# Setup of a graph layer reordered: row credits first, statistics in a row, node turns over six banks

## The chip, the cores and the metric

The kernel runs on one core of a Trainium2 chip. The metric is the time of one execution in microseconds (us), the median of the runs shown. Before the change it is 634.7 us (three runs, 634.36 to 635.47).

The engines of the core are named as in the profile: PE is TensorE, DVE is VectorE, ACT is ScalarE, POOL is GpSimd, SP is SyncE. PEld is TensorE's weight load. A name with a "q" (DVEq, POOLq) is that engine's instruction queue at work on registers, semaphores or DMA issues rather than on data.

## The reference

A graph layer (a message per edge, summed at its target node, then two dense layers with batch normalisation) is followed by a mixture of 16 experts. Only the first part matters here:

```python
x0 = layernorm(x)                              # x: 1250 nodes x 512
msg = relu(x0[src] + edge_attr @ W_e + b_e)    # 21250 edges, edge_attr: 21250 x 64
aggr = segment_sum(msg, dst, num_segments=1250)
h = (1.0 + eps) * x0 + aggr
h = silu(batchnorm(h @ W1 + b1, g1, beta1))    # W1: 512 x 1024
h = h @ W2 + b2                                # W2: 1024 x 512
x = x + silu(batchnorm(h, g2, beta2))
# then experts: gate, top 156 tokens for each of 16 experts, two dense layers each, weighted sum
```

The edges come sorted by `dst`. Source nodes are arbitrary, so rows of `x0` are gathered.

## The kernel before

Each engine has a program of its own, in the order in which it is written, and the programs meet at semaphores. An engine does its instructions strictly in that order, so whatever waits holds up all that stands behind it on the same engine.

**Setup.** SP issues the loads of `x` in five groups of two tiles (125 rows each), then `W_e`, the first block of edge attributes and `eps`. ACT issues the loads of `dst` (two forms), `src` and the bias `b_e` (`be_all`). Per group `g` of two tiles: `statistics(g)` on DVE (L812: two BN_STATS, two BN_AGGR), `deviations(g)` on ACT (L540, a square root), `norm_terms(g)` on DVE (L823: reciprocal and mean term), `normalise(g)` on ACT (L545, two tiles into `xn`), `table(g)` on DVE (L830: 64 times `xn` plus scaled bias, written over `xs`), and then SP writes these rows to `node_rows` in DRAM (L366 to L370). ACT's order is `deviations(g+1)` ahead of `normalise(g)`. On DVE the five groups follow one another nearly whole: `statistics(2)` stands behind `table(0)`, `statistics(3)` behind `table(1)`, `statistics(4)` behind `table(2)` (L843 to L887). `statistics(1)` stands behind the scaling of `be_all` (L845), which waits for that load.

Between these, DVE works out from `dst` where each block of edges begins (`sb_base`, `shift`, `base_i`) and whether one pass over the edges is enough (`n_pass`, through `outside`, `n_out`, a product on PE at L1287 and `pass_ready`). With the data here one pass is run.

The normalised nodes are also turned (features by nodes) into `aggT`, times 1 + eps. PE turns tile `t` into `bank[t % 2]` (`node_transposes`, L1275), even tiles are copied by ACT (L558 to L562) and odd ones by DVE (`node_columns`, L890). Both copies stand behind the last step of the tables on their engine, and tile `t` of PE waits for the copy of tile `t - 2`. Then the small vectors `vecA`, `vecB` are turned (L1290 to L1292) and copied by DVE (L899, L900). SP issues their loads and that of `gate_s` behind the writes of `node_rows`; the four loads of `W1` (0.5 MB each) follow them (L366 to L381).

**Edge steps.** There are 34 steps of five tiles of 128 edges, 167 tiles in all. For tile `t`: POOL gathers 128 rows of `node_rows` into `row(t)`, one of 26 places (L474); PE computes `edge_attr @ W_e` for two tiles at a time into PSUM (`edge_pair`, L1316); DVE adds the gathered row (L952); ACT applies relu into `msg` (L599); PE sums the messages into a window of 64 nodes with a one-hot matrix (`fold`, L1300). Per step ACT copies the sum (`sum_copy`, L574), PE turns it (`turn_sum`, L1308) and DVE adds it into `aggT` at a column that it reads from memory (`accumulate`, L905):

```python
dve.wait_ge(sum_turned, 1 + w * SB + (i + 1))
dve.wait_ge(acc_done, 1 + w * SB + i)
base = dve.value_load(base_i[0:1, bass.ds(w * SB + (i + 2), 1)], min_val=0, max_val=N - 1)
```

DVE does `accumulate(i - 1)` between its fourth and its fifth add of step `i`. In steps 4 to 7 ACT and DVE each also split a quarter of `W1` into two halves (`W1_high` L579, `W1_low` L929). In steps 10 to 33, PE computes one of 24 partial products with `W1` per step (`part_product`, L1337), ACT copies it out (`part_copy`, L586, line L589) and DVE takes its statistics (`part_statistics`, L939, line L942).

POOL may gather a row when `node_rows` is complete (`tab_out`), `pass_ready` is given, and `row_used` allows it. The first increment of `row_used` comes from DVE (L973), as the last thing ahead of its edge steps:

```python
dve.sem_inc(row_used, 1)
dve.sem_inc(acc_done, 1)
run_steps(dve, n_pass, SB, step)
```

## Time and profile before

| | us |
|---|---|
| median of three runs | 634.7 |
| the profiled execution, whole | 632.95 |
| its span, first to last instruction | 631.0 |
| first edge product of PE starts | 43.15 |
| edge steps end (last sum added) | about 301 |
| batch normalisation, second layer, experts | the remaining 330 |

Rows of the trace give the start of an instruction in us from the span's start and its duration. "[idle before <-releaser]" is how long the engine sat idle just ahead of it, and what ended that. The chain of waits is followed back from the last instruction, at each step to what released it; only time on it sets the end.

### The profile page before, as it was taken

How to read it: one execution, taken by the hardware profiler on the slowest of the kernel's cores; microseconds unless marked ns; L12 is line 12 of the kernel's file. 1: busy time of each engine (PE TensorE's matmuls, PEld its weight loads, DVE VectorE, ACT ScalarE, POOL GpSimd, SP SyncE). 2: the span in 40 equal slices, each digit the busy share in tenths (PEclk: the TensorE clock that was granted, in tenths of full speed). 3: DMA queues.
4: the chain of work that ended last, by engine and by line, in shares of the span. 5: the costliest groups of instructions: out<-in, count | busy, mean ns of one | idle time of the engine just before them, and what ended most of it. 6: DMA issues, size and time to landing. Idle time of an engine off the chain costs nothing.

```text
span 631.0 us, 11762 instructions
## 1 busy us (share of the span) xinstructions
PE 495.0 (78%) x4023; PEld 318.0 (50%) x4023; DVE 392.5 (62%) x961; ACT 324.2 (51%) x660; POOL 255.9 (41%) x245
## 2 busy tenths in 40 slices
PE   1068866799989998998899976811499999999990
PEld 1032221233434333334446535610499999999990
DVE  4747655666666675765579746577747666675530
ACT  2425544555554554554486219534046676675750
POOL 2027777777777765400000000000334655556431
PEclk9977978899999998999999997755589999999995
DMA  9487777777777775611667505740058999984331
GB/s 219 122 276 235 225 220 217 221 227 229 228 230 219 219 220 170 188 43 58 211 220 187 157 0 184 232 178 0 21 152 254 299 278 270 302 234 64 60 41 21
DMA packets 48944, 112.44 MB, mean 178 GB/s; under 512 B 7145, under 2 KB 7565, under 8 KB 48886
## 3 DMA queue, kind: packets, MB, share of 16 engines
q0 software_dynamic: 18992, 54.02, 31.6%
q1 hardware_dynamic: 29399, 57.16, 29.0%
q10 hardware_dynamic: 494, 0.52, 0.4%
q8 instruction: 32, 0.52, 0.3%
q14 instruction: 27, 0.21, 0.1%
HBM read 98.88 MB, written 12.79 MB: 177 GB/s over the span
## 4 chain that ended last, share of the span: by engine, by line
PE 62%; DVE 13%; ACT 10%; issue 6%; DMA 3%; DVEq 3%; POOL 1%; SPq 1%; ACTq 1%; POOLq 0%
PE bank L1333 19%; PE bank L1514 11%; PE bank L1303 10%; PE bank L1324 8%; DVE bank L952 4%; ACT big L599 3%; PE bank L1540 2%; PE bank L1312 2%; DVEq L909 2%; PE bank L1495 2%; PE bank L1504 1%; DVE rows_z L1154 1%; PE bank L1383 1%; DMA big<-in_L_gnn_b_e 1%; ACT rows_z L680 1%
## 5 line engine op out<-in xcount | busy, mean ns | idle before, releaser
L1303 PE MATMUL bank<-big,edge_home 128*64 128x256 f32 x668 | 111.5, 426 | 35.2 <-ACT big L599 35.2
L599 ACT ACTIVATE big<-bank 128x512 f32<-128x512 f32 x167 | 99.5, 596 | 71.7 <-DVE bank L952 68.4
L484 POOL DMA_INDIRECT big<-token_rows,idx x32 | 37.6, 1174 | 221.9 <-DVE idx L1212 214.5
L474 POOL DMA_INDIRECT pair<-node_rows,edge_home x97 | 96.3, 992 | 34.6 <-issue 28.0
L1333 PE MATMUL bank<-big,pair 128*128 128x156 f16 (+2 forms) x1056 | 106.5, 260 | 1.1 <-DVE big L1011 0.9
L1333 PEld LDWEIGHTS bank<-big,pair 128*128 128x128 f16 x1056 | 80.9, 97 | 24.5 <-issue 1.4
L474 POOL DMA_INDIRECT big<-node_rows,edge_home x70 | 67.8, 969 | 62.3 <-DVEq L973 37.9
L1303 PEld LDWEIGHTS bank<-big,edge_home 128*64 128x64 f32 x668 | 35.8, 142 | 93.5 <-issue 58.5
L1324 PE MATMUL bank<-edge_home 64*128 64x512 f16 x501 | 74.0, 403 | 3.4 <-DVE edge_home L926 3.4
L493 POOL DMA_INDIRECT out<-rows_z,idx x32 | 51.0, 1593 | 45.2 <-issue 26.3
L952 DVE TENSOR_TENSOR bank<-pair,bank 128x512 f32<-128x512 f32 x97 | 64.3, 687 | 6.1 <-PE bank L1324 5.3
L952 DVE TENSOR_TENSOR bank<-big,bank 128x512 f32<-128x512 f32 x70 | 46.5, 688 | 11.2 <-PE bank L1324 6.4
L912 DVE TENSOR_TENSOR aggT<-bank,aggT 128x256 f32 x34 | 14.4, 425 | 52.3 <-PE bank L1312 50.9
L731 ACT ACTIVATE big<-bank,colB 128x156 f32<-128x156 f32 x64 | 21.5, 388 | 46.2 <-PE bank L1514 46.2
L1324 PEld LDWEIGHTS bank<-edge_home 64*128 64x128 f16 x501 | 18.5, 97 | 49.5 <-issue 37.1
L1333 PE MATMUL bank<-rows_z 128*128 128x250 f16 x288 | 35.8, 273 | 0.0
L1333 PEld LDWEIGHTS bank<-rows_z 128*128 128x128 f16 x288 | 26.5, 98 | 12.5 <-issue 9.7
L1514 PE MATMUL bank<-big,raw 128*128 128x156 f32 x192 | 29.9, 313 | 0.5 <-ACT big L725 0.5
L1200 DVE TENSOR_SCALAR big<-iota_slot,slot 125x156 f16<-125x156 f16 x160 | 28.8, 265 | 0.0
L589 ACT ACTIVATE xs_home<-bank,colA 128x250 f32<-128x250 f32 x18 | 8.5, 470 | 39.4 <-PE bank L1333 39.4
L1514 PEld LDWEIGHTS bank<-big,raw 128*128 128x128 f32 x192 | 27.9, 202 | 0.8 <-ACT big L725 0.8
L1280 PE MATMUL bank<-ident,rows_z 125*128 125x125 f32 x40 | 8.8, 383 | 20.9 <-ACT aggT L560 12.6
(222 smaller groups left out, 778.5 us busy)
## 6 DMA issues: line engine op xcount, KB each, us to landing
raw<-in_L_ffn_w SPq DMA_DIRECT2D x12, 1024.0 KB, 8.5
edge_home<-in_L_ffn_w SPq DMA_DIRECT2D x6, 1024.0 KB, 8.2
pair<-in_L_ffn_w SPq DMA_DIRECT2D x6, 1024.0 KB, 9.7
edge_home<-in_edge_attr SPq DMA_DIRECT2D x19, 320.0 KB, 4.1
xs_home<-in_x SPq DMA_DIRECT2D x10, 448.0 KB
xs_home<-in_L_ffn_w SPq DMA_DIRECT2D x4, 1024.0 KB, 8.2
aggT<-in_L_ffn_w SPq DMA_DIRECT2D x4, 1024.0 KB, 10.6
node_rows<-xs_home SPq DMA_DIRECT2D x5, 448.0 KB
```

Of the source, the lines that this page charges most:

```text
L474: pool.indirect_dma_start(row(t), None, node_rows, bass.IndirectOffsetOnAxis(src_i[:, t:t + 1], 0)).then_inc(row_in[t % RR], 16)
L484: pool.indirect_dma_start(xg[e % XR][:, a, :], None, token_rows, bass.IndirectOffsetOnAxis(idx[:, e, a:a + 1], 0)).then_inc(xg_in[e % XR], 16)
L493: pool.indirect_dma_start(out, bass.IndirectOffsetOnAxis(idx[:, e, a:a + 1], 0), yw[e % YR][:, a, :], None, compute_op=ALU.add).then_inc(y ...
L599: act.activation(msg[:, t % MR, :], bank[t % PB][0:Q, :], ACT.Relu, scale=1.0 / E_SCALE).then_inc(msg_ready, 1)
L731: act.activation(h32[e % 2][:, f, :], bank[2 + half][:, f % 2 * K:(f % 2 + 1) * K], ACT.Gelu_apprx_tanh, bias=colB[:, e * HK + f:e * HK + ...
L912: dve.tensor_tensor(window, bank[6 + i % 2][:, 0:HK * WIN] .rearrange("p (k a n) -> p a k n", k=HK // 2, a=2), window, ALU.add).then_inc(a ...
L952: dve.tensor_tensor(bank[t % PB][0:Q, :], row(t), bank[t % PB][0:Q, :], ALU.add).then_inc(row_used, 1)
L1200: last = dve.tensor_scalar(pick[e % 2][:, t, :], iota_slot[:], slot[:, e, t:t + 1], None, ALU.is_equal)
L1303: done = pe.matmul(bank[6 + b][a * WIN:(a + 1) * WIN, 0:H // 2], onehot[b][:, j, :], msg[:, t % MR, a * (H // 2):(a + 1) * (H // 2)], star ...
L1324: last = pe.matmul(bank[t % PB][0:Q, :], attr16[u % 2][side, i, c * Q:(c + 1) * Q], We16[side, j, :], start=(p == 0), stop=(p == 2), skip_ ...
L1333: last = pe.matmul(bk, weights(i, k), values(j, k), start=(begin and p == k == 0), stop=(end and p == 2 and k == n - 1), skip_group_check= ...
L1514: last = pe.matmul(bank[2 + half][:, f % 2 * K:(f % 2 + 1) * K], e32[e % RH][:, 0, k, f * 128:(f + 1) * 128], xT[e % 2][:, k, :], start=(k ...
```

## The change

The diff is cut to what differs in work or order. Renamed constants (`FG`, `HB`, `PAIRS`, `ZSTART`, `part_at`) have the values that stood there as numbers (2, 256, 5, steps 9, 17, 25), so the schedule of the partial products is the same; `W1` is split one step earlier (steps 3 to 6). Tables for later passes (`shift` and `base_i` for 20 further passes) are gone; the values are remade at the start of a pass by `bases(w)`.

```diff
@@ SP: small loads ahead of the writes of node_rows
+            for v, k in ((b1, F1), (g1, F1), (beta1, F1), (b2, HK), (g2, HK), (beta2, HK)):
+                sp.dma_start(vecA[o:o + k, :], v.rearrange("(k p) -> k p", p=128)).then_inc(vec_in, 16)
+            sp.dma_start(vecB[0:EX * HK, :], ...); sp.dma_start(vecB[EX * HK:, :], ...)
+            sp.dma_start(gate_s[:], gate_t).then_inc(vec_in, 16)
             for g in range(NT // XG):
                 sp.wait_ge(tab_ready, g + 1)
...
             for u in range(1, AR):
                 load_attr(u)
-            (the same nine loads)
             for k in range(HK):
                 sp.dma_start(W1_32[:, k, :], W1_t[:, k, :]).then_inc(w1_in, 16)
@@ POOL
-            pool.iota(shift[:, SB:], [[WIN, NWIN + 1], [0, SB]], base=0, channel_multiplier=0,
+            pool.iota(pass_add[:, 1:], [[WIN, NWIN]], base=0, channel_multiplier=0,
-            pool.iota(base_i[:, 2 + SB:2 + SB * (1 + NWIN)], ...); two memsets of base_i
+            three memsets of pass_add and pass_mul
@@ ACT and DVE, node columns; PE, node transposes
-                               bank[t % 2][:, 0:HK * P]
+                               bank[NB[t % 6]][:, 0:HK * P]        # NB = (0, 1, 2, 5, 6, 7)
-                if t >= 2:
-                    pe.wait_ge(xt_sb[t % 2], t // 2)
+                if t >= 6:
+                    pe.wait_ge(xt_sb[t % 2], (t - 6) // 2 + 1)
-            for t in range(2):
+            for t in range(5):
                 node_transposes(t)
             pe.wait_ge(base_ready, 7)
@@ DVE, setup
+            def be_scaled():
+                dve.wait_ge(be_in, 32)
+                dve.tensor_scalar(be_all, be_all, E_SCALE, None, ALU.mult).then_inc(be_in, 1)
+            dve.sem_inc(row_used, 1)
+            dve.sem_inc(acc_done, 1)
             dve.wait_ge(sorted_in, 32)
...
             statistics(0)
-            dve.wait_ge(be_in, 32)
-            dve.tensor_scalar(be_all, be_all, E_SCALE, None, ALU.mult)
             dst_f copy
+            statistics(1)
             norm_terms(0)
             early
-            dve.wait_ge(iotas, 9)
             dve.wait_ge(base_ps, 1)
-            dve.tensor_copy(base_i[0:1, 2:2 + SB], bank[3][0:1, 0:SB])
             dve.tensor_copy(shift[:, 0:SB], bank[3][0:Q, 0:SB]).then_inc(base_ready, 1)
-            statistics(1), outside, norm_terms(1), outside >= WIN, table(0), n_out, statistics(2), n_out + early,
-            norm_terms(2), table(1), n_pass_f, statistics(3), n_pass_i, norm_terms(3), table(2), dst_left,
-            statistics(4), norm_terms(4), table(3), eps1, dst_left, memset aggT, table(4)
+            statistics(2), norm_terms(1), outside, statistics(3), norm_terms(2), be_scaled, outside >= WIN,
+            wait be_in 33, table(0), statistics(4), norm_terms(3), n_out, table(1), norm_terms(4), n_out + early,
+            table(2), n_pass_f, table(3), n_pass_i, table(4), dst_left, eps1, dst_left, memset aggT,
+            wait iotas 10
             node_columns(1), (3), (5), (7), (9)
@@ DVE, edge steps
             def accumulate(w, i):
+                base = dve.value_load(base_i[0:1, i:i + 1], min_val=0, max_val=N - 1)
                 dve.wait_ge(sum_turned, 1 + w * SB + (i + 1))
                 dve.wait_ge(acc_done, 1 + w * SB + i)
-                base = dve.value_load(base_i[0:1, bass.ds(w * SB + (i + 2), 1)], min_val=0, max_val=N - 1)
...
+            def bases(w):
+                dve.tensor_scalar(shift[:], shift[:], pass_mul[:, bass.ds(w, 1)], pass_add[:, bass.ds(w, 1)],
+                                  ALU.mult, ALU.add).then_inc(based, 1)
+                dve.wait_ge(based, w * 2 + 1)
+                dve.tensor_copy(base_i[:], shift[0:1, :]).then_inc(based, 1)
+                dve.wait_ge(based, w * 2 + 2)
             def columns_hot(w, i):
-                                         scalar=shift[:, bass.ds(w * SB + i, 1)],
+                                         scalar=shift[:, i:i + 1],
             def step(w, i):
                 if i == 0:
+                    bases(w)
                     columns_hot(w, 0)
...
-            dve.sem_inc(row_used, 1)
-            dve.sem_inc(acc_done, 1)
             run_steps(dve, n_pass, SB, step)
```

## Rows read from the trace of the kernel before

**Rows 1.** Busy time by stage: start:end, length, PE, PEld, DVE, ACT, POOL, clock, DMA, GB/s.
```profile
0.00:16.40 16.40, 2.49 (x10) 2.04 (x10) 7.48 (x28) 3.31 (x6) 3.26 (x14) 1.00 0.92 218
...
43.20:77.10 33.90, 28.19 (x182) 9.55 (x182) 20.62 (x34) 17.11 (x31) 25.88 (x27) 0.84 0.80 252
77.10:114.60 37.50, 25.69 (x149) 8.11 (x147) 22.10 (x34) 18.25 (x31) 28.97 (x29) 0.83 0.73 212
...
130.60:300.50 169.90, 154.04 (x1124) 65.92 (x1121) 109.29 (x197) 90.96 (x173) 95.77 (x99) 0.98 0.62 185
```

**Rows 2.** Chain of waits, setup: start, us, what held the end.
```profile
3.17 7.75 DMA big<-in_L_gnn_b_e
...
30.61 1.09 DVE xs_home L833
...
37.01 2.17 DMA gate_s<-in_L_ffn_gate_weight
...
40.94 0.89 issue
...
43.30 4.97 DMA big<-node_rows,edge_home
```

**Rows 3.** Timeline of DVE in the setup: start, us, line, operation.
```profile
6.33 1.27 DVE L817 BATCH_NORM_STATS2 stats<-xs_home 125x6 f32<-125x512 f32 x2
7.63 0.25 DVE L820 BATCH_NORM_AGGREGATE mean_var<-stats 125x2 f32<-125x6 f32 x2
10.95 0.43 DVE L845 TENSOR_SCALAR big<-big 125x512 f32<-125x512 f32 x1 [3.07 <-DMA big<-in_L_gnn_b_e]
...
27.49 0.17 DVE L826 RECIPROCAL rstd<-std 125x2 f32<-125x2 f32 x1 [0.27 <-ACT std L542]
...
30.53 1.16 DVE L833 SCALAR_TENSOR_TENSOR xs_home<-rows_z,big 125x1024 f32<-125x1024 f32 x1
...
38.85 0.74 DVE L892 TENSOR_SCALAR aggT<-bank,eps 128x500 f32<-128x500 f32 x1 [0.80 <-PE bank L1280]
...
42.28 0.82 DVE L926 TENSOR_TENSOR edge_home<-edge_home 128x640 f16<-128x640 f32 x1
```

**Rows 4.** Timeline of ACT in the setup, one group of two tiles.
```profile
18.18 0.20 ACT L542 ACTIVATE std<-mean_var 125x2 f32<-125x2 f32 x1 [3.01 <-DVE mean_var L820]
18.30 1.50 ACT L549 ACTIVATE rows_z<-xs_home,shift_mean,rstd 125x512 f32<-125x512 f32 x2
```

**Rows 5.** Timeline of PE: turns of six node tiles, and the first edge products.
```profile
32.48 5.37 PE L1280 MATMUL bank<-ident,rows_z 125*128 125x125 f32 x24 [0.37 <-DVE aggT L892]
...
43.15 2.74 PE L1324 MATMUL bank<-edge_home 64*128 64x512 f16 x12 [3.43 <-DVE edge_home L926]
```

**Rows 6.** Line L467 in POOL's queue, right behind the wait for `node_rows`: ns, start.
```profile
L467 POOLq TENSOR_LOAD <-n_pass_i x1: 507/507/507, 36.3 to 36.3; - x1
```

**Rows 7.** Timeline, POOL's 1st, 24th, 31st gather; DVE waiting for one.
```profile
41.83 1.16 POOL L474 DMA_INDIRECT big<-node_rows,edge_home  x1 [37.92 <-DVEq L973]
...
71.31 0.95 POOL L474 DMA_INDIRECT pair<-node_rows,edge_home  x1 [0.31 <-issue]
...
74.69 1.35 DVE L952 TENSOR_TENSOR bank<-pair,bank 128x512 f32<-128x512 f32 x2 [0.60 <-DMA pair<-node_rows,edge_home]
...
80.22 1.58 POOL L474 DMA_INDIRECT big<-node_rows,edge_home  x1 [0.30 <-issue]
```

**Rows 8.** Chain of waits in step 7, around the sum's way into `aggT`.
```profile
104.00 0.63 PE bank L1312 x2
...
105.47 0.07 DVE aggT L912
```

**Rows 9.** Timeline of ACT, DVE and PE in a step with a partial product.
```profile
145.74 0.47 ACT L589 ACTIVATE xs_home<-bank,colA 128x250 f32<-128x250 f32 x1 [1.57 <-PE bank L1333]
...
146.25 0.42 DVE L942 BATCH_NORM_STATS2 st<-xs_home 128x6 f32<-128x250 f32 x1
...
148.02 0.65 PE L1303 MATMUL bank<-big,edge_home 128*64 128x256 f32 x4 [0.40 <-ACT big L599]
```

More of the change, by code:

```diff
@@ L47, in gnn_ffn_kernel @@
     ZPARTS = 3
-    ZSTEPS = 8
-    ZHEAD = SB - ZPARTS * ZSTEPS
+    SLOPE, OFFSET = 33.0, 14.0
+    ZSTART = (9, 17, 25)
+    ZOFF = (0, 1, 2, 3, 4, 5, 6, 7)
+    ZLAG = 0
+    assert all(s * SLOPE - OFFSET >= (c + 1) * ZC for c, s in enumerate(ZSTART))
+    part_at = {ZSTART[q // F1] + 1 + ZOFF[q % F1]: q for q in range(ZPARTS * F1)}
+    assert max(part_at) + ZLAG < SB and all(max(ZOFF) + 1 + ZLAG + s <= z for s, z in zip(ZSTART, ZSTART[1:]))
+    W1_FIRST = ZSTART[0] - 6
     YC = [(0, 250), (250, 375), (625, 625)]
@@ L225, in gnn_ffn_kernel @@
         silu = [aggT[:, i, 0:CH[2][1]] for i in range(HK)]
-        half = 2 * J * H
+        half = MR * H
         rows = big[0:Q, 0:half].rearrange("p (s h) -> p s h", h=H)
@@ L236, in row @@
             s = t % RR
-            return rows[:, s, :] if s < 2 * J else late_rows[(s - 2 * J) // 8][:, (s - 2 * J) % 8, :]
+            return rows[:, s, :] if s < MR else late_rows[(s - MR) // 8][:, (s - MR) % 8, :]
         msg = big[0:Q, half:2 * half].rearrange("p (s h) -> p s h", h=H)
@@ L566, in _ @@
             act.wait_ge(pass_ready, 1)
-            n_pass = act.value_load(n_pass_i[0:1, 0:1], min_val=1, max_val=2 + NWIN)
+            n_pass = act.value_load(n_pass_i[0:1, 0:1], min_val=1, max_val=1 + NWIN)
             def attr_high(w, u):
@@ L886, in _ @@
             dve.memset(aggT[:, :, N:], 0.0)
-            table(4)
+            dve.wait_ge(iotas, 10)
             dve.wait_ge(eps_ready, 1)
@@ L956, in step @@
                         accumulate(w, i - 1)
-                    if j == 4 and i % 2 == 0 and i // 2 + 1 < NU:
-                        attr_low(w, i // 2 + 1)
-                if i >= ZHEAD:
-                    part_statistics(w, i - ZHEAD)
-                c, u = divmod(i + 1 - ZHEAD, ZSTEPS)
-                if u == 0 and 0 <= c < ZPARTS:
-                    part_low(w, c)
-                if ZHEAD - 2 - HK <= i < ZHEAD - 2:
-                    W1_low(w, i - (ZHEAD - 2 - HK))
+                    if t % (2 * PAIRS) == 4 and t // (2 * PAIRS) + 1 < NU:
+                        attr_low(w, t // (2 * PAIRS) + 1)
+                if i - ZLAG in part_at:
+                    part_statistics(w, part_at[i - ZLAG])
+                if i in ZSTART:
+                    part_low(w, ZSTART.index(i))
+                if W1_FIRST <= i < W1_FIRST + HK:
+                    W1_low(w, i - W1_FIRST)
                 if i == SB - 1:
@@ L1287, in _ @@
             pe.matmul(bank[3][0:1, 64:65], ones[0:Q, 0:1], n_out[:], start=True, stop=True).then_inc(base_ps, 1)
-            for t in range(2, NT):
+            for t in range(5, NT):
                 node_transposes(t)
@@ L1297, in _ @@
             pe.wait_ge(pass_ready, 1)
-            n_pass = pe.value_load(n_pass_i[0:1, 0:1], min_val=1, max_val=2 + NWIN)
+            n_pass = pe.value_load(n_pass_i[0:1, 0:1], min_val=1, max_val=1 + NWIN)
             def fold(t, j, last, b):
-                for a in range(2):
-                    done = pe.matmul(bank[6 + b][a * WIN:(a + 1) * WIN, 0:H // 2], onehot[b][:, j, :],
-                                     msg[:, t % MR, a * (H // 2):(a + 1) * (H // 2)],
+                for a in range(FG):
+                    done = pe.matmul(bank[6 + b][a * WIN:(a + 1) * WIN, 0:HB], onehot[b][:, j, :],
+                                     msg[:, t % MR, a * HB:(a + 1) * HB],
                                      start=(j == 0), stop=(j == last), skip_group_check=True)
@@ L1310, in turn_sum @@
                 pe.wait_ge(sum_out, w * SB + (i + 1))
-                for k in range(HK // 2):
+                for k in range(HB // 128):
                     last = pe.transpose(bank[6 + i % 2][:, k * 128:(k + 1) * 128], fold_sum[:, k * 128:(k + 1) * 128],
@@ L1361, in step @@
                         turn_sum(w, i - 1)
-                    if j == min(2, last) and i >= ZHEAD:
-                        part_product(w, i - ZHEAD)
+                    if j == min(2, last) and i in part_at:
+                        part_product(w, part_at[i])
                 if i == SB - 1:
```

123 lines of the change are left out of this document (63 added, 60 removed).

## The prediction

> **What bounds the kernel now.** I read the busy time by stage first, then the chain of waits through the setup, then each engine's timeline there, and last single steps of the edge stage. Three stretches matter; all behind 301 us is the same program.
>
> The setup, up to about 47 us, has no engine at its limit. The chain goes through the load of `b_e`, then the tables up to 31.70, then the small loads up to 39.18, then an issue gap and the first gather [rows 2]. POOL's first gather had waited 37.92 us for DVE's L973, given only at the end of DVE's setup, although `node_rows` was complete at 36.3 [rows 6, 7].
>
> The first edge steps are paced by the gathers. The 24th starts at 71.31, the first at 41.83, so one takes 29.48 / 23 = 1.28 us, 6.4 us per step of five; and at 74.69 DVE had idled 0.60 us for a gathered row [rows 7]. PE is busy 28.19 of 33.90 us there, at a mean granted clock of 0.84: part of it at 1.2 instead of 2.4 GHz [rows 1].
>
> Later the steps are paced by PE (154.04 of 169.90 us busy, clock 0.98), with the split of `W1` between, where PE has 25.69 of 37.50 us [rows 1].
>
> **Part 1, DVE's setup.** Costs: statistics of a group 1.27 + 0.25, about 1.55 us with the gap; norm terms two instructions near 0.17, some 0.4; a table about 1.2; the scaling of `b_e` 0.43 [rows 3]. ACT needs 0.20 for a deviation and 1.50 for a group's normalisation [rows 4]. The small steps for `n_pass` I put at 0.1 to 0.3 each, as the reciprocal beside them.
>
> Statistics of group 0 start at 6.33 as before. The statistics now wait for `x` alone. No row shows when each group lands. The bound from below is that each is there when its group before was done; the bound from above is 16.4 us for all five, since the first 16.40 us move 218 GB/s, 3.6 MB, which holds the 2.56 MB of `x` and about 1 MB of other loads [rows 1]. With `x` first in SP's queue I take 11, 13.3 and 15.7 us for groups 2 to 4. Then, by addition: statistics 1 end at 9.6; statistics 2 wait to 11, end 12.7; statistics 3 end 14.9; scaled `b_e` and the small steps to 15.8; table 0 ends at 17.0 (behind it queue statistics 4 and all other tables); statistics 4 end 18.5, table 1 at 20.2, table 2 at 21.7, table 3 at 22.95, table 4 at 24.2. ACT is never late for one: its last normalisation runs 20.6 to 22.1. Before, the last table ended at 30.53 + 1.16 = 31.69 [rows 3]. Tables end 7.5 us earlier: table 0 hardly moves, but the five no longer alternate with statistics and ACT.
>
> PE now does five turns ahead of the product for `n_pass`. Their last tile is normalised near 16.1 and turned by about 17.1; `n_out` is there only at 20.6, so this wait delays nothing. `pass_ready` comes near 23, ahead of `node_rows`. The wait for `iotas` stands late on DVE, behind work that ends at 25, and POOL's own set-up of constants is no longer than before.
>
> **Part 2, rows written and row credits.** The last table ended at 31.69 and POOL passed its wait at 36.3, 4.6 us later [rows 3, 6]. Now the last three tables come 1.25 us apart instead of about 1.6 for the last two, while 0.51 MB takes about 1.9 us even at 275 GB/s, so the writes queue by some 0.9 us more; an estimate from the stage rates of 218 to 252 GB/s [rows 1], taken somewhat over them because writes are alone for a while. `node_rows` is then complete at 24.2 + 4.6 + 0.9 = 29.7. With the credit given at the start, POOL goes on at once: 36.3 to 37.25 for reading `n_pass`, as its 0.51 us load plus as much of register work [rows 6], and 0.89 from credit to gather [rows 2], together 1.9. First gather at 31.6 instead of 41.83: **10.2 us earlier**. Bounds: 11.4 if the writes queue no more than 0; 5 if `W1` (next part) gets in their way.
>
> The nine small loads now pass the ten writes in SP's queue, and are issued while SP waits for table 0 anyway. The last of them, `gate_s`, which held the chain at 37.01 for 2.17 us [rows 2], is then long there. `W1`'s 2 MB were issued right behind it, some 4 us ahead of the first gather; now they come right behind the writes and an attribute block, at about 26 to 28, again some 4 us ahead. So the first gather's wait for its row, from 43.30 for 4.97 us [rows 2], is kept: 48.27 less 10.2 is 38.1 for the second row, and one gather earlier, about 36.6, for the first, whose add is then the first of the stage (before, near 46.8 by the same step back).
>
> **Part 3, is anything else later than 36.6?** ACT and DVE copy turned nodes from about 24.7 on. Six tiles are turned by then; tiles 6 to 9 wait for the copies of 0 to 3, at 5.37 / 6 = 0.9 us a tile [rows 5]: 25.4 to 29.1. DVE's copy of tile 9 (0.74) ends at 29.9. Before, that copy began at 38.85, and the first edge product at 43.15 [rows 3, 5]; the same 4.3 us behind 29.15 gives 33.5. `bases(0)` adds two small instructions with a wait for each on DVE, ahead of the one-hot of step 0 and of `attr_low` for which PE waits: 0.3 to 0.9 us; I take 0.6, as two of the reciprocal's kind with its gap [rows 3]. PE's first products run from 34.1; the first pair is half of 2.74 us [rows 5], ready at 35.5. The gathered row at 36.6 is last, by about 1 us. So the turns over six banks and `bases` cost and bring nothing by themselves; if that cover went, each us of it would count.
>
> The first steps then stay paced by the gathers at 1.28 us a tile, so the 10.2 us are kept but not raised, and the value load's gain is nothing there. `W1` one step earlier swaps one such step with a later normal one of like length.
>
> Beside DVE at work a gather is slower: the first took 1.16 us, beside DVE's L926 (42.28), and the one at 80.22 took 1.58, both against 0.95 [rows 3, 7]. An earlier first gather meets DVE's tail in the same way; 0.2 of this is in the rows carried over, up to 0.6 more is possible, and I take none. The Trainium skill, SBUF — State Buffer, section "SBUF: two separate sides", goes further and speaks against the change: while DVE runs an instruction of the two-port kind, GpSimd is locked out of a shared port and can't write the descriptors of its DMAs. By that the first gather would wait for DVE's last setup instructions, which is a rival below; by the rows it waits a fraction of one.
>
> **Part 4, the column's load.** Before, the sum was turned at 104.63 and added at 105.47: 0.84 us, most of it the load of the column behind the wait [rows 8]. With the load ahead of the wait, and DVE idle for the turn, some 0.25 is left: 0.6 us per step where that is on the chain. That holds in the four `W1` steps, where add, relu, `W1_high`, `W1_low` and the next adds follow one another: 2.4 us. It holds for the last sum: 0.6. In the 24 steps with a partial product it mostly doesn't: the statistics at 146.25 start 0.04 us after ACT's copy ended (145.74 + 0.47 = 146.21), and that copy waited for PE [rows 9]. DVE could come 0.6 us earlier and would wait for ACT instead. I take 0 there; bounds 0 to 0.40 us per two steps, PE's idle time in that pattern [rows 9], so 0 to 4.8. The dynamic column of the one-hot saves a register instruction per step, on the chain in a few: 0.3 in all.
>
> **Sum.** 10.2 + 2.4 + 0.6 + 0.3 = 13.5 us. Against the profiled execution, 632.95 - 13.5 = 619.45; the median lies 1.75 above it, so the forecast is 621.2.
>
> **Rivals.**
> *The load counts in the product steps too.* For it: PE does idle 0.40 there behind DVE and ACT [rows 9]. Against: ACT's copy ends at the same moment. Time: 621.2 - 4.8 = 616.4.
> *The writes of `node_rows` become the bound.* Five writes that come closer and 2.4 MB of attributes and `W1` directly behind them. For: the DMA engines were 0.92 busy at 218 GB/s already in the first stage [rows 1]. Against: `W1` is behind them in the same queue, and before, an attribute block stood behind the last write as well. If they share half and half from 26 us, 1.2 MB left to write take up to 11 us instead of 5.5: gather 5 us later, 626.
> *The order brings nothing, only the credit does.* If the tables end where they did, the gather starts at 36.3 + 1.9 = 38.2, but PE's first product stays at 43.15 and the first pair is ready at about 44.5, 2.3 earlier than 46.8. With part 4: 634.7 - 2.3 - 3.3 = 629.1.
> *DVE's tail holds up the gathers.* For: 1.16 and 1.58 us beside DVE [rows 7]. Against: these are parts of one DVE instruction, not whole ones. If POOL waited for two and a half instructions like L926 (0.82) [rows 3], 2.0 us: 623.2. The Trainium skill's lock (part 3) is this mechanism.
> *Slower: the clock.* The product steps ran at 0.98; the stages before at 0.83 and 0.84, where PE idles more [rows 1]. If a shifted setup and `W1` split left PE at 0.84 there, 154.04 x (0.98 / 0.84 - 1) = 25.7 us would be lost: 646.9. It decides from 13.5 us, a clock of 0.90. Against: the steps' own idle of 0.40 us is unchanged, and what fell before lay in the stages with long waits.
>
> **How the numbers follow.** Forecast 0.55 (its own range 619 to 623, by the writes' 1.2 us either way and the unseen landings); load everywhere 0.14; writes 0.16; DVE's tail 0.05; credit only 0.06; clock 0.04. The range 614.5 to 626 leaves out the last two, half of the writes' case and a little below. A measurement tells about 0.2% (1.3 us) here; all cases but the clock are faster by more: faster 0.95, same 0.01, slower 0.04.
>
> **What would show it.** Right: last table near 24, POOL's L467 near 30 and first gather near 31.6, with no wait for DVE; first add near 36.6, just at a row's landing; the gap from turn to `aggT` about 0.25; DVE's L942 now waiting for ACT in every product step; edge steps ending near 287.5. Wrong: L467 over 32 (writes), a first add behind PE instead of a gather, product steps shorter than 14.0 us a pair, or a clock under 0.95 in them.

## The result and the profile after

The changed kernel takes 614.46 us in the median of four runs (609.34 to 615.58), the one before 635.09 in the runs beside it (634.36 to 637.05): a ratio of 0.966 with a 95% interval of 0.960 to 0.972. The forecast was 621.2 with a range from 614.5, so the time lies a hair under the low end. The profiled execution took 615.38 us, span 613.57, against 632.95 and 631.0 before.

To see where the 17.4 us between the two spans come from, I cut both at the adds of the turned sums into `aggT` (34 instructions, DVE L912 before and L928 after; step *k* is the time from the start of add *k* - 1 to that of add *k*):

| stretch, us | before | after | gain | forecast |
|---|---|---|---|---|
| start to add 0 | 58.55 | 48.60 | 9.95 | 10.2 |
| the four ordinary steps among 1 to 8 | 24.91 | 22.50 | 2.41 | 0 |
| the four steps that split `W1` (4 to 7 before, 3 to 6 after) | 37.48 | 32.69 | 4.79 | 2.4 |
| step 9, in which `aggT` is first split | 9.61 | 8.41 | 1.20 | 0 |
| steps 10 to 33, nearly all with a partial product | 169.97 | 170.54 | -0.57 | 0.9 |
| behind add 33 (same program) | 330.48 | 330.83 | -0.35 | 0 |
| sum | | | 17.4 | 13.5 |

The setup came out as forecast; the steps between it and the partial products gave 8.4 us instead of 2.4. The same stages in the busy times of the changed kernel, cut at its own adds (columns as in [rows 1]):

```profile
0.00:16.40 16.40, 5.00 (x21) 4.11 (x22) 10.19 (x35) 6.75 (x12) 1.58 (x14) 1.00 0.93 221
28.50:37.30 8.80, 2.98 (x13) 0.78 (x13) 3.21 (x8) 1.25 (x2) 5.53 (x5) 0.68 1.02 387
37.30:59.60 22.30, 19.86 (x124) 6.86 (x126) 16.39 (x27) 13.14 (x24) 16.92 (x18) 0.82 0.78 235
59.60:92.30 32.70, 23.15 (x150) 7.71 (x148) 22.11 (x35) 18.35 (x31) 25.38 (x25) 0.91 0.72 213
92.30:112.20 19.90, 16.89 (x116) 5.75 (x116) 13.86 (x23) 11.96 (x21) 15.32 (x16) 0.93 0.75 222
112.20:282.80 170.60, 155.56 (x1129) 66.49 (x1127) 109.60 (x198) 90.97 (x173) 103.61 (x106) 0.98 0.64 192
282.80:613.60 330.80, 263.67 (x2452) 220.84 (x2452) 205.94 (x613) 175.41 (x387) 88.97 (x64) 0.88 0.56 161
```

The fourth line is the stretch of the four `W1` steps: granted clock 0.91, where the like stretch before had 0.83 [rows 1]. PE's clock has two levels, so a mean of 0.91 over 32.7 us is 2 x 0.09 x 32.7 = 5.9 us at 1.2 GHz, against 2 x 0.17 x 37.5 = 12.8 before. In the first 16.4 us DVE is busy 10.19 us instead of 7.48: the statistics moved there.

The setup's DVE, from its timeline (start, us, line, and in brackets the idle time before it with what ended it):

```profile
22.33 1.21 DVE L844 SCALAR_TENSOR_TENSOR xs_home<-rows_z,big 125x1024 f32<-125x1024 f32 x1
...
28.31 0.74 DVE L908 TENSOR_SCALAR aggT<-bank,eps 128x500 f32<-128x500 f32 x1 [0.93 <-PE bank L1302]
...
30.05 0.69 DVE L995 SCALAR_TENSOR_TENSOR edge_home<-edge_home 128x512 f16<-128x512 f32 x1 [0.70 <-ACT edge_home L630]
30.66 0.30 DVE L933 TENSOR_SCALAR edge_home<-edge_home 128x34 f32<-128x34 f32 x1
30.99 0.17 DVE L936 CAST edge_home<-edge_home 1x34 int32<-1x34 f32 x1
...
31.77 0.82 DVE L950 TENSOR_TENSOR edge_home<-edge_home 128x640 f16<-128x640 f32 x1
37.31 0.70 DVE L977 TENSOR_TENSOR bank<-big,bank 128x512 f32<-128x512 f32 x1 [4.72 <-DMA big<-node_rows,edge_home]
```

The last table ends at 23.54 (31.69 before [rows 3]); the last node copy at 29.05; the first add of a gathered row starts at 37.31, after 4.72 us of waiting for the row and for nothing else. The chain of waits says the same (start, us, what held the end):

```profile
24.95 3.50 DMA node_rows<-xs_home
...
28.53 0.51 POOLq L479
...
29.55 0.90 issue
30.44 6.85 DMA big<-node_rows,edge_home
...
37.31 0.71 DVE bank L977
```

POOL passes its wait for `node_rows` at 28.5 and reaches its first gather at 30.44, with nothing from DVE between; before, it stood there for 37.92 us until DVE's credit [rows 7]. The first two gathers take 1.34 and 1.35 us and the third 0.95, the pace of all later ones:

```profile
30.44 1.34 POOL L486 DMA_INDIRECT big<-node_rows,edge_home  x1 [28.21 <-issue]
32.08 1.35 POOL L486 DMA_INDIRECT big<-node_rows,edge_home  x1 [0.30 <-issue]
33.74 0.95 POOL L486 DMA_INDIRECT big<-node_rows,edge_home  x1 [0.30 <-issue]
```

Around a sum's way into `aggT`, the chain is now short: 0.12 us from the end of the turn to the add, where it was 0.84 [rows 8].

```profile
75.39 0.38 PE bank L1334 x2
...
75.89 0.07 DVE aggT L928
```

### The profile page after: what moved, and what is told of

Read it like the earlier page. It is cut to its first block, busy times and chain, and to the rows that moved or that the text cites. A ratio compares the mean times of both kernels' runs of the same rounds, so it can differ in the third digit from the quotient of the medians.

```text
span 613.6 us, 11694 instructions
## 1 busy us (share of the span) xinstructions
PE 492.7 (80%) x4023; PEld 317.0 (52%) x4023; DVE 391.9 (64%) x961; ACT 324.5 (53%) x660; POOL 257.3 (42%) x245
## 4 chain that ended last, share of the span: by engine, by line
PE 63%; DVE 11%; ACT 9%; DMA 5%; issue 5%; POOL 2%; DVEq 1%; SPq 1%; POOLq 0%; ACTq 0%
PE bank L1355 22%; PE bank L1536 11%; PE bank L1325 11%; PE bank L1346 7%; ACT big L611 3%; DVE bank L977 3%; PE bank L1562 2%; PE bank L1334 2%; PE bank L1526 2%; PE bank L1517 2%; POOL pair L486 1%; DVE rows_z L1176 1%; PE bank L1399 1%; PE bank L1405 1%; DMA xs_home<-in_x 1%
## 5 line engine op out<-in xcount | busy, mean ns | idle before, releaser
L1325 PE MATMUL bank<-big,edge_home 128*64 128x256 f32 x668 | 109.4, 420 | 30.9 <-ACT big L611 30.5
L486 POOL DMA_INDIRECT big<-node_rows,edge_home x70 | 70.5, 1006 | 49.3 <-issue 48.3
L977 DVE TENSOR_TENSOR bank<-pair,bank 128x512 f32<-128x512 f32 x97 | 64.1, 687 | 6.2 <-PE bank L1346 6.1
L977 DVE TENSOR_TENSOR bank<-big,bank 128x512 f32<-128x512 f32 x70 | 46.5, 687 | 11.5 <-PE bank L1346 6.0
L928 DVE TENSOR_TENSOR aggT<-bank,aggT 128x256 f32 x34 | 14.4, 424 | 27.4 <-PE bank L1334 27.4
L966 DVE BATCH_NORM_STATS2 st<-xs_home 128x6 f32<-128x250 f32 x18 | 7.6, 421 | 26.5 <-ACT xs_home L601 26.5
```

What stands on the lines that cost most here:

```text
L486: pool.indirect_dma_start(row(t), None, node_rows, bass.IndirectOffsetOnAxis(src_i[:, t:t + 1], 0)).then_inc(row_in[t % RR], 16)
L928: dve.tensor_tensor(window, bank[6 + i % 2][:, 0:HK * WIN] .rearrange("p (k a n) -> p a k n", k=HB // 128, a=FG), window, ALU.add).then_in ...
L977: dve.tensor_tensor(bank[t % PB][0:Q, :], row(t), bank[t % PB][0:Q, :], ALU.add).then_inc(row_used, 1)
L1325: done = pe.matmul(bank[6 + b][a * WIN:(a + 1) * WIN, 0:HB], onehot[b][:, j, :], msg[:, t % MR, a * HB:(a + 1) * HB], start=(j == 0), stop ...
```

## The experiments

**The theory** after the result: two independent causes. The setup's reordering is worth some 10 us, as forecast. The load of the column's number ahead of the wait (the prediction's Part 4) is worth as much again, because it shortens every step up to the 9th and, by cutting PE's idle time there, leaves PE longer at its full clock. **The rivals**: the setup brought more than the table above shows and the load only its 3.3 us; or the place of the `W1` split, one step earlier, did it. Times are medians against the kernel before on the same chip (635.25, 633.19 and 634.04 in the three groups); places are starts in the one profiled execution of each kernel, in us.

| run | median us | ratio, 95% interval | first gather | first add | add 2 | add 9 | add 33 |
|---|---|---|---|---|---|---|---|
| before | 635.1 | | 41.83 | 46.84 | 71.01 | 130.55 | 300.52 |
| after | 614.46 | 0.966 (0.960 to 0.972) | 30.44 | 37.31 | 59.60 | 112.20 | 282.75 |
| e1 load ahead, in before | 625.38 | 0.985 (0.979 to 0.990) | 41.65 | 46.84 | 70.66 | 125.20 | 292.34 |
| e2 load behind, in after | 624.87 | 0.982 (0.980 to 0.985) | 30.97 | 37.38 | 60.98 | 121.86 | 290.61 |
| e3 credit only, in before | 633.97 | 0.999 (0.997 to 1.001) | 38.13 | 45.50 | 69.45 | 127.68 | 296.39 |
| e4 two banks (one run) | 612.37 | | 31.13 | 37.53 | 60.77 | 114.20 | 281.22 |
| e5 `W1` split a step later | 615.64 | 0.967 (0.962 to 0.971) | 29.96 | 36.98 | 58.56 | 114.81 | 283.33 |
| e6 old order on DVE | 622.26 | 0.980 (0.972 to 0.988) | 37.44 | 43.82 | 66.02 | 120.55 | 289.11 |
| e7 small loads behind (one run) | 613.04 | | 30.75 | 37.95 | 59.57 | 112.61 | 282.49 |
| e8 `W1` loaded later | 616.24 | 0.974 (0.967 to 0.980) | 30.33 | 34.29 | 63.11 | 115.08 | 283.64 |
| e9 fillers, in after | 610.68 | 0.963 (0.958 to 0.967) | 31.50 | 36.90 | 60.78 | 111.62 | 278.86 |
| e10 e2 and fillers | 621.00 | 0.977 (0.971 to 0.983) | 30.55 | 36.50 | 61.12 | 116.88 | 284.21 |
| e11 `W1`'s loads spread | 617.87 | 0.973 (0.969 to 0.978) | 30.63 | 34.14 | 64.54 | 116.55 | 286.49 |
| e12 e11 and fillers | 614.61 | 0.970 (0.966 to 0.974) | 31.17 | 34.69 | 63.65 | 113.19 | 280.20 |

### The load of the column, alone and undone

e1, in the kernel before:

```diff
+                base = dve.value_load(base_i[0:1, bass.ds(w * SB + (i + 2), 1)], ...)
                 dve.wait_ge(sum_turned, 1 + w * SB + (i + 1))
                 dve.wait_ge(acc_done, 1 + w * SB + i)
-                base = dve.value_load(base_i[0:1, bass.ds(w * SB + (i + 2), 1)], ...)
```

> The kernel before, with one edit: the load of the column stands ahead of the two waits of accumulate. Theory A (the forecast's terms for this load are right, 2.4 us in the W1 steps, 0.6 at the end, nothing in the product steps; the rest of the unforeseen gain comes from the setup): about 3.3 us less than before, near 631.5. Theory B (the load is what shortened steps 3 to 9 by 6.9 us in the changed kernel, part of it by a higher granted clock): 6 to 8 us less, near 628, with the W1 steps at about 8 us each instead of 9.4, and the granted clock of that stretch over 0.83. By both the first gather stays at 41.8.

e2 is the reverse edit in the changed kernel, with the index by register as it was.

> The changed kernel, with the load of the column behind the waits again, at an address worked out from the pass as before (the places of later passes aren't filled; one pass is run). Theory A: 3.3 us more than the changed kernel. Theory B: 6 to 8 us more, with the W1 steps back at about 9.4 us and a granted clock near 0.83 in steps 3 to 9. The setup up to the first add at 37.3 unchanged by both.

The load is worth 635.25 - 625.38 = 9.9 us alone and 624.87 - 614.46 = 10.4 us undone; the other edits together, from before to e2, 635.25 - 624.87 = 10.4. The two add up to the whole, so the setup did not bring more than was forecast, and the load brought three times its 3.3 us. e2's chain in an early step shows the mechanism:

```profile
53.41 0.38 PE bank L1334 x2
...
53.92 0.32 DVEq L925
...
54.27 0.19 DVEq L925
...
54.64 0.07 DVE aggT L928
...
54.99 0.69 DVE bank L977
...
55.70 0.61 ACT big L611
...
56.35 0.68 PE bank L1325 x4
```

DVE works in order. While it stands at the wait for the turned sum and then loads (53.79 to 54.64), the add of the next gathered row (L977) is queued behind it, then ACT's relu, then the fold that PE needs. PE runs dry: the chain passes turn, load, add, relu and fold in each of steps 1, 2, 7 and 8, 6.1 to 6.3 us long, and no gather is on it. With the load ahead these steps take 5.4 to 5.8 us, and only now do gathers enter the chain, as in these lines of the changed kernel's, which stand for ten gathers in a row:

```profile
47.62 0.95 POOL pair L486
...
48.88 0.95 POOL pair L486
...
59.37 3.67 DMA pair<-node_rows,edge_home
```

From 38 us to add 9 POOL's gathers are 12% of the changed kernel's chain and none of e2's, whose chain has 6% in the load instead.

How much these steps gain depends on the gathers. With the load behind the wait, the four ordinary steps take 24.9 us in each of the four profiled runs (before, e2, e3, e10), and no gather is on the chain between add 0 and add 8. With it ahead, and `W1`'s loads in front of the first gather, they take 22.5 to 25.2 us in seven runs; the change has the shortest, and e1 the longest. In e1 the chain is nothing but gathers, one behind the other, from the first at 41.65 to the row that lands at 75.80:

```profile
70.26 0.95 POOL pair L474
...
71.52 4.28 DMA pair<-node_rows,edge_home
...
77.24 0.07 DVE aggT L912
```

So alone, in the kernel before, the load brings nothing up to add 3 (77.24 against 77.12): the gathers stand right behind it as the next bound. In the changed kernel add 2 starts 29.16 us behind the first gather, before 29.18, in e1 29.01, in e2 30.01. The load ahead is what lets the steps keep up there with a first gather that comes 11.4 us earlier.

Nor does e1's trace show its whole gain where the load acts. Against the kernel before it is 4.4 us shorter from add 0 to add 9 and 0.9 earlier at add 0, but also 2.8 shorter in steps 10 to 33 and 1.8 behind add 33.

### The setup, edit by edit

e3 gives the row credits first and changes nothing else of the kernel before:

```diff
+            dve.sem_inc(row_used, 1)
+            dve.sem_inc(acc_done, 1)
             dve.wait_ge(sorted_in, 32)
...
-            dve.sem_inc(row_used, 1)
-            dve.sem_inc(acc_done, 1)
             run_steps(dve, n_pass, SB, step)
```

> The kernel before, with the two first credits given at the start of DVE's program and nothing else. The forecast's rival on this: first gather at 38.2 instead of 41.8, first add at 44.5 (then PE's first pair is last), 2.3 us less. A theory that the credit is the main part of the setup's gain: first add 3.6 us earlier or more.

The credit alone is worth little: the median is 1.28 us under that of before in its group, with an interval that includes no gain at all, and in the trace add 0 comes 58.55 - 56.99 = 1.56 us earlier. POOL's first gather comes 3.7 us earlier, at 38.13, and the row still lands only at 45.50, as the timelines of POOL and DVE show:

```profile
38.13 1.16 POOL L474 DMA_INDIRECT big<-node_rows,edge_home  x1 [34.22 <-issue]
...
45.50 0.69 DVE L954 TENSOR_TENSOR bank<-big,bank 128x512 f32<-128x512 f32 x1 [2.49 <-DMA big<-node_rows,edge_home]
```

That is 7.4 us for a row that took 5.0 before. The first product, at 43.07 as before, had been ready; the row was last.

e6 puts DVE's old order of statistics, tables and small steps back into the changed kernel:

```diff
             statistics(0)
+            be_scaled()
...
-            statistics(1)
             norm_terms(0)
...
-            table(4)
+            norm_terms(4)
...
+            table(3)
...
             dve.memset(aggT[:, :, N:], 0.0)
+            table(4)
```

> The changed kernel with DVE's setup in the order of before (statistics and tables of the groups one after the other, bias scaled early), credits still first, six banks kept. Forecast: the order is what makes the tables end 8 us earlier; last table near 31, POOL's wait ends near 35.5, first gather near 37.5, the whole 6 to 7 us slower than the changed kernel. Rival (the credit and the banks carry the gain): within 2 us of it.

The last table then ends at 31.28 and the first gather starts at 37.44; the time rises by 7.8 us, the edge stage's end by 6.4:

```profile
30.12 1.16 DVE L844 SCALAR_TENSOR_TENSOR xs_home<-rows_z,big 125x1024 f32<-125x1024 f32 x1
...
37.44 1.17 POOL L486 DMA_INDIRECT big<-node_rows,edge_home  x1 [35.20 <-issue]
```

So the order on DVE carries most of the setup's gain. The new order without the early credit was not run. In the changed kernel the credit's old place, behind L995, is reached at 30.05 + 0.69 = 30.74; with the 0.90 us from there to the gather the first gather would start near 31.6 instead of 30.44, so by this estimate the credit is worth some 1.2 us there too.

e4 turns the nodes over two banks again (`bank[t % 2]` for `bank[NB[t % 6]]`, two turns ahead of the product for `n_out` instead of five), and e7 moves the nine small loads behind the writes of `node_rows`.

> The changed kernel with the nodes turned over two banks again. Forecast: PE turns tiles 2 to 9 only after 24, about 0.97 us each, so turns end near 32.5 and PE's first edge product moves from 32.65 to about 36.8; its first pair is then ready at about 38.2, 0.9 us behind the first row at 37.3: 0.9 us slower. Rival (the banks are hidden altogether): no difference.

> The changed kernel with the nine small loads behind the writes of node_rows again. Forecast: gate_s lands near 32, PE turns the vectors then instead of at 28.2, first edge product near 36.5, first pair ready near 37.9; but W1 is issued 4.4 us later, so the first rows come about 2 us sooner, near 35.5. First add near 38, 0.6 us later than in the changed kernel. Rival (small loads are no more on the way): first add earlier, near 36.

PE's first product moves from 32.65 to 35.94 and 36.36, and the first add only to 37.53 and 37.95. But the cover is used up in both, since the first add now waits for PE. The first row lands 4.9 us after its issue in e4, near 36.0, and 7.0 us in e7, near 37.8. e4's lines:

```profile
35.94 2.74 PE L1346 MATMUL bank<-edge_home 64*128 64x512 f16 x12 [3.93 <-DVE edge_home L950]
...
37.53 1.29 DVE L977 TENSOR_TENSOR bank<-big,bank 128x512 f32<-128x512 f32 x2 [1.65 <-PE bank L1346]
```

So the first add comes 1.5 us behind its row in e4 and 0.2 in e7. Add 0 is no later than in the changed kernel (47.92 and 48.38 against 48.60), and their times, 612.37 and 613.04 in one run each, lie within the spread of the changed kernel's own.

### The `W1` split's place and the loads of `W1`

e5 splits `W1` one step later, as before (`W1_FIRST = ZSTART[0] - 5`).

> The changed kernel with W1 split in steps 4 to 7, as before, instead of 3 to 6. Forecast: one gather-paced step swaps with a normal one, no difference (within 1 us). Theory C (the earlier split is what shortened steps 3 to 9, since PE has three normal steps instead of two ahead of the first product step, and its clock rises in them): 3 us or more slower, with the granted clock between the W1 steps and the first product step lower.

615.64 with nearly the same interval as the change: this edit can't be told from nothing, so it is not where most of the gain came from.

e8 takes `W1`'s four loads from ahead of the first gather and issues them when the first rows are used; e11 issues them one by one, behind rows 2, 5, 8 and 11:

```diff
             n_pass = sp.value_load(n_pass_i[0:1, 0:1], min_val=1, max_val=1 + NWIN)
+            for k in range(HK):
+                sp.wait_ge(row_used, 3 + 3 * k)
+                sp.dma_start(W1_32[:, k, :], W1_t[:, k, :]).then_inc(w1_in, 16)
```

> The changed kernel, with the four loads of W1 issued by SP after six rows have been used, instead of right behind the writes of node_rows. Theory A (the first gathers are slowed by these 2 MB: first row 6.85 us after its issue in the changed kernel, 7.4 with the credit alone, 5.0 before): the first row lands about 4 us after its issue, first add near 34.5, some 2 to 2.5 us less in the end. Rival (the row waits for something else, such as DVE's tail beside the gather): first add stays at 37.3, no difference. By both, W1 is there before step 3.

> The changed kernel with the four loads of W1 (512 KB each) issued one by one, behind the rows 2, 5, 8 and 11 of the edge loop, instead of in front of the first gather. Theory (the first gathered row took 6.85 us to land because W1's loads were under way, and all four behind the first rows only moved the collision into step 1): the first row lands in 4 to 4.5 us, the first add starts at 34.3 to 35, and step 1 keeps 5.4 to 6.5 us, so that accumulate 2 starts 1.5 to 3 us earlier (57 to 58) and the edge loop's end at 280 to 281.5. Rival (each load holds a gather up by itself, so the delay is only spread over steps 1 and 2): first add at 34.3 to 35, and accumulate 2 at 59 to 61, the loop's end within 1 us of 282.8.

Without `W1` beside it the first row lands after 3.8 us (e8) or 3.5 (e11) instead of 6.85, and the first add comes 3 us earlier (in e8 it then waits for PE). By add 2 it is all given back: add 2 starts 3.5 us later than in the changed kernel in e8, 4.9 in e11, which was to gain and lost the most. The DMA issues between 30 and 66 us (KB each, median us from issue to landing) show it, in the changed kernel:

```profile
edge_home<-in_edge_attr SPq DMA_DIRECT2D x3, 320.0 KB, 5.4
pair<-node_rows,edge_home POOLq DMA_INDIRECT x16, 3.7
```

and in e11:

```profile
raw<-in_L_gnn_W SPq DMA_DIRECT2D x4, 512.0 KB, 5.9
edge_home<-in_edge_attr SPq DMA_DIRECT2D x3, 320.0 KB, 6.9
pair<-node_rows,edge_home POOLq DMA_INDIRECT x16, 5.4
```

The median of these 16 gathers into `pair` goes from 3.7 to 5.4 us, and DVE waits for rows, as in these lines of e11, where its timeline in the changed kernel shows no wait for a row between 39 us and add 2:

```profile
47.36 0.70 DVE L978 TENSOR_TENSOR bank<-big,bank 128x512 f32<-128x512 f32 x1 [2.29 <-DMA big<-node_rows,edge_home]
...
51.43 0.70 DVE L978 TENSOR_TENSOR bank<-pair,bank 128x512 f32<-128x512 f32 x1 [1.20 <-DMA pair<-node_rows,edge_home]
```

My theory of the spreading fell; its rival (each load holds gathers up by itself) was right in kind and too mild. In front of the first gather, the loads delay one row by 2.9 us while PE has nothing else; inside the stage they delay many. In the medians, 1.8 and 3.4 us above the change, neither run is clear of it: the intervals overlap.

### The clock, apart from the load

e9 adds matmuls that compute nothing to the `W1` steps, e10 the same to e2, e12 to e11:

```diff
+                if W1_FIRST <= i < W1_FIRST + HK:
+                    for _ in range(6):
+                        pe.matmul(bank[PB][:, 0:512], We16[:, 0, 0:128], We16[:, 0, :], start=True, stop=True)
                 if i == SB - 1:
                     turn_sum(w, i)
```

> The changed kernel, with six matmuls of 512 columns added on PE at the end of each of the four steps in which W1 is split, into a bank that nothing reads (1.3 us of PE at full clock, against 2.1 to 2.9 us of PE idle time in each of those steps). They compute nothing and serve to leave PE shorter idle pieces. Clock theory (about half of what the early column load won in these steps came from a higher granted clock, 8.8 us of half clock between accumulates 2 and 9 instead of 17.1): half clock in this stretch falls to 0 to 4 us, the four steps fall from 32.7 us to 29 to 31.5, the edge loop's end (accumulate 33, 282.8) comes 1 to 3 us earlier. Rival (these steps are held by VectorE's and ScalarE's work, and the clock only follows their waits): the four steps stay at 32 to 35 us, later where the added matmuls lie in the way of a fold, and the time stays at 614 to 618.

> The changed kernel with the column load put back behind the waits (as in the run before with that edit alone, which was at 624.9; the column's number is again read where it isn't filled for later passes, which don't run here) and the same six matmuls in each of the four W1 steps. That run had these four steps at 38.6 us with 17.1 us of half clock between accumulates 2 and 9. Clock theory: with the clock held up the four steps come down by 2.5 to 3.5 us to about 35 to 36, with half clock under 7 us; what stays above the changed kernel's 32.7 is the load's own place, about 3 us. Rival (the load alone): the four steps stay at 38 to 39 us whatever the clock, and the time at 624 to 626.

> Both edits, W1's loads one by one behind the rows 2, 5, 8 and 11 and the six matmuls in each of the four W1 steps. If the two causes are separate, the gains add: the edge loop's end at what the better of the two reaches less the other's gain, 278 to 281, and the time 610 to 613. If the clock is what both act on, no more than the better one alone.

Together with the change and e2 this is a square of two by two over the four `W1` steps (for the change, the fourth line of its busy times above). The busy times of these steps in e2:

```profile
61.00:99.60 38.60, 26.02 (x148) 8.15 (x142) 22.14 (x34) 18.07 (x30) 29.76 (x30) 0.83 0.72 214
```

In e10, and under it steps 10 to 33:

```profile
61.10:94.70 33.60, 26.37 (x176) 9.06 (x172) 22.10 (x34) 18.06 (x30) 26.29 (x25) 1.00 0.72 209
...
116.90:284.20 167.30, 151.44 (x1125) 65.25 (x1122) 108.93 (x197) 90.88 (x173) 99.39 (x103) 1.00 0.65 194
```

The same two stretches in e9:

```profile
60.80:91.50 30.70, 25.25 (x166) 8.87 (x166) 22.07 (x34) 18.16 (x31) 24.00 (x22) 1.00 0.71 208
...
111.60:278.90 167.30, 152.29 (x1129) 65.58 (x1128) 109.64 (x198) 90.91 (x173) 106.30 (x107) 1.00 0.67 198
```

| four `W1` steps, us (clock) | no fillers | fillers | what the clock takes |
|---|---|---|---|
| load behind the wait | 38.6 (0.83) | 33.6 (1.00) | 5.0 |
| load ahead | 32.7 (0.91) | 30.7 (1.00) | 2.0 |
| what the load takes | 5.9 | 2.9 | |

At full clock the load is worth 2.9 us here, close to the forecast's 2.4; a single such step takes 7.7 us in e9 and 8.4 in e10. In these four executions the other 3.0 of its 5.9 go with the clock: with it behind the wait, the same stretch pays 5.0 us for the lower level instead of 2.0. But each cell is one execution, and without fillers the clock of these steps scatters: with the load ahead 0.80 (e5) to 0.95 (e8), at 31.7 to 34.9 us in eight runs; with it behind 0.83 to 0.88, at 36.0 to 38.6 us in three. So the 2.9 us are shown; that the load's place raises the clock is not. The rival, that these steps are held by DVE and ACT whatever the clock, fell in both rows. The second lines of e10 and e9 settle the question of the partial-product steps: 167.3 us with the load behind and 167.3 with it ahead, at clock 1.00 in both.

Nor is the clock of the `W1` steps what makes the load worth three times its forecast: with fillers in both kernels, and the clock at 1.00 there, the medians still differ by 621.00 - 610.68 = 10.3 us. The two traces differ by 8.1 us: 1.0 ahead of add 0, 4.2 from there to add 9 (2.9 of it in the `W1` steps), 0.1 in steps 10 to 33 and 2.8 behind add 33.

The fillers lower the median in all three pairs: e2 to e10 by 3.9 us, e11 to e12 by 3.3, the change to e9 by 3.8 (by the ratios, which take out the difference between the groups: 3.6, 2.1 and 1.8 us). The intervals overlap within each pair, so that no pair alone shows the fillers to be faster; e9, 610.68 us, has the lowest ratio of all. With the clock held up, the gathers are the next bound: they are 32% of e9's chain from 38 us to add 9. e12 stays above e9: the gains of spreading and fillers do not add, since the spreading had none.

## Why the prediction missed, step by step

**The setup (Parts 1 to 3), 10.2 us: right in sum, by two errors inside that happen to cancel.** The tables end at 23.54, forecast 24.2; POOL reads `n_pass`, right behind its wait for `node_rows`, 5.0 us behind them (28.53), forecast 5.5, so five closer writes queued by 0.4 us instead of 0.9 and the rival of the writes (626) did not come. From there to the gather 1.9 us, as forecast. The first gather is thus 1.2 us early. Its row, however, took 6.85 us and not the 5.0 that I carried over [rows 2]: first add 37.31, forecast 36.6. `W1`'s 2 MB were under way in both kernels. Without them the row takes 3.5 to 3.8 us (e8, e11, e12); with them 4.9 to 7.3 in the eleven other runs, 5.4 in e9, whose program is the changed kernel's up to there. So a single row's landing could not be carried over. The prediction had `W1` only as a bound of 5 for the gather's start. e3's 1.56 us at add 0, where the rival "credit only" had 2.3, is the same error.

**DVE beside the gathers.** The first two gathers took 0.4 us more than the 0.95 of the others, beside DVE's L995 to L950. The prediction had up to 0.6 as possible and took none. The Trainium skill, SBUF — State Buffer, section "SBUF: two separate sides", would have had GpSimd locked out while DVE runs an instruction of the two-port kind; the trace agrees in direction, at 0.4 us each, and shows no gather standing still for all of an instruction. Whether L995 to L950 are of that kind, no row says.

**Six banks, small loads, `bases` and the `W1` step: right in the time, as far as runs show.** Neither e4, e7 nor e5 has a time that can be told from the change. The cover named in Part 3 was real, but without the banks or the early small loads it is gone: the first add then waits for PE (e4, e7). `bases` was not run apart; its two instructions (L933, L936, from 30.66 to 31.16) lie under the same cover.

**The ordinary steps and step 9 (Part 3's end): the step that failed.** The prediction said that the first steps "stay paced by the gathers" and that the load's gain "is nothing there"; steps 8 and 9 got no term at all. The pace of the gathers (1.28 us a row, 6.4 us a step [rows 7]) and that of the steps (6.1 to 6.3) coincided, and I took the equality for a cause on the strength of one 0.60 us wait. The chain of waits of the kernel before has the load in DVE's queue (L909) in each of these steps, and no gather between add 0 and add 3:

```profile
57.81 0.33 DVEq L909
...
63.95 0.32 DVEq L909
...
70.29 0.31 DVEq L909
```

I had read that chain only in the setup and in step 7 [rows 2, 8]. Measured, four ordinary steps gave 2.41 us and step 9 another 1.20, where the forecast had 0; undone (e2), these five steps lose 3.8 us. With fillers in both (e10 against e9) they lose 1.3. The gathers were not far off as a bound: e1, the load alone, gains nothing in the first three steps, and its chain there is gathers. That the change gains 1.5 us in steps 1 and 2 fits its add 2 coming 11.41 us earlier, as much as the first gather (11.39): the load gone from the path, the steps keep up with the earlier gathers. In the forecast's sum the load's term, 2.4 + 0.6 + 0.3 = 3.3 us, is the one that failed: it measured 9.9 to 10.4 us in the medians.

**The `W1` steps (Part 4), 2.4 us: right at full clock, mis-sized where the clock moves.** The load itself is 2.9 us there (e9 against e10); the profiled executions gave 4.79, and 5.9 between e2 and the change. The rival named "the clock" let it move only against the change; a gain in clock, 3.0 of these 5.9 us, had no term. As the clock of these steps scatters from 0.80 to 0.95 with the load ahead, part of the 4.79 is luck of the executions profiled. The rows for it stood there: 0.83 and 0.84 in exactly the stretches where PE idles [rows 1].

**The partial-product steps, 0 us: right.** A pair of steps takes 14.0 us before and after. As said, DVE now comes early and waits for ACT's copy there, where the statistics stood with no idle time before [rows 9]:

```profile
143.37 0.42 DVE L966 BATCH_NORM_STATS2 st<-xs_home 128x6 f32<-128x250 f32 x1 [0.64 <-ACT xs_home L601]
```

The rival "the load counts in the product steps too" gave 616.4, near the time, but in the wrong place: it had 4.8 us there and they gave none. The 0.57 us by which steps 10 to 33 were longer are small beside what the clock does there: 167.3 at 1.00, 170.6 at 0.98. The last sum's 0.6 us and the registers' 0.3 did not show: at equal clock the whole stretch is alike to 0.1 us.

**Profile and median.** The forecast put the median 1.75 us above the profiled execution, as before; here it lies 0.92 below. Of the 6.7 us between forecast and median, 4.1 are steps (17.6 gained in the profiled execution instead of 13.5) and 2.7 this. Single runs of the changed kernel spread over 6.2 us, and their clock differs too (0.910 and 0.918 at 613.6 and 613.8 us of span, 0.926 at 611.0, 0.932 at 607.3).

**Left open.** The load is worth some 10 us in the medians, alone, undone and with fillers, but between add 0 and add 9, where it acts, the traces show 4.4 (e1), 9.7 (e2 against the change) and 4.2 us (e10 against e9). The rest lies elsewhere in the traces, and its cause stays open. Part of it is at the end: behind add 33 every kernel here runs the same instructions, yet the three other profiled runs with the load behind took 331.7 (e10), 333.2 (e3) and 333.3 us (e2) there, the kernel before 330.5 and the ten with the load ahead 328.7 to 330.8. It makes some 2.5 of the 10.4 us of the load in e2. What differs is the time at 1.2 GHz: for e2 2 x 0.13 x 333.3 = 87 us by its row, for the change 2 x 0.12 x 330.8 = 79:

```profile
290.60:623.90 333.30, 266.61 (x2452) 223.96 (x2452) 205.96 (x613) 175.43 (x387) 88.17 (x64) 0.87 0.54 158
```

Why the clock of this stage should depend on an edit in the stage before it, or whether that is chance in few profiles, the runs don't settle.

## What to carry to other kernels

Where a stage seems paced by a transfer whose pitch equals its step, follow the chain of waits through an ordinary step before believing it: an engine that waits in order with a register load behind the wait holds up all that is queued after it, and moving 0.7 us ahead of the wait was worth 10 us in the median, 4 to 10 of them in nine steps by the traces. Then try that edit alone: here the gathers were the next bound, so close behind that the first three steps gained nothing by it in the kernel before. When an edit shortens PE's idle time in a stretch with a clock under 1.00, give the clock a term with both signs, priced from the same stretch at either level. A bulk load was cheaper here where one thing waits for it: 2 MB ahead of the first gather cost the first add 3 us, the same 2 MB among the gathers made add 2 come 3.5 to 4.9 us later than that.

## What the runs showed of the hardware

- Matmuls that compute nothing, put into idle time of PE, shortened the steps they were added to: 38.6 to 33.6 and 32.7 to 30.7 us, with the granted clock going from 0.83 and 0.91 to 1.00 (one profiled execution each).
- Indirect gathers of rows slow down beside bulk loads: a median of 3.7 us from issue to landing for 16 of them in the changed kernel, 5.4 us with four loads of 512 KB spread among the gathers (e11). The first row takes 4.9 to 7.3 us right behind the same loads (eleven runs), 3.5 to 3.8 without them (three).
- POOL's gather needed 1.34 instead of 0.95 us beside DVE's work in the setup.
- With a register load behind the wait in DVE's queue, 0.84 us passed from the end of the turn to the add; with the load ahead of the wait, 0.12.
